# Attention scores of two heads side by side in 64-row halves, in six steps a group, with the value products in one piece

## What is computed

```python
# first layer, L0_attn and L0_ffn
xn = _layernorm(x, axis=-1)
qkv = jnp.einsum('btd,ed->bte', xn, w_qkv)          # 16 heads of 16 channels
scores = jnp.einsum('bqhd,bkhd->bhqk', q, k) * SCALE
scores = scores + causal_bias                       # -10000 above the diagonal
attn = jax.nn.softmax(scores, axis=-1)
out = jnp.einsum('bhqk,bkhd->bqhd', attn, v)
s = jnp.einsum('btd,ed->bte', out.reshape(b, t, D_OUT), w_out)
g = _silu(FFN(xn))                                  # gate, up, down with int weights
x = x + s * g
# second layer: a long convolution (by transforms) and a mixture of 20 experts with the best 2 of each token
```

## Time and profile before

| | us |
|---|---|
| median of 3 runs | 1039.91 (1037.98 to 1041.28) |
| the profiled execution | 1047.65, its span 1045.9 |
| PE busy | 954.6 (91%) |
| weight loads | 720.9 (69%) |
| DVE busy | 685.5 (66%) |
| ACT busy | 467.8 (45%) |
| POOL busy | 327.5 (31%) |
| mean granted clock of PE, as a share of full speed | 0.955 |

### The profile page before, as it was taken

How to read it: one execution, slowest core, us unless ns; L and a number is a source line. 1 busy time by engine, 2 the same in 40 slices (tenths; PEclk the granted TensorE clock), 3 DMA queues, 4 the chain that set the end, 5 groups by cost and what they waited for, 6 DMA issues and landing times.

```text
span 1045.9 us, 18938 instructions
## 1 busy us (share of the span) xinstructions
PE 954.6 (91%) x5844; PEld 720.9 (69%) x5844; DVE 685.5 (66%) x1451; ACT 467.8 (45%) x871; POOL 327.5 (31%) x605
## 2 busy tenths in 40 slices
PE   8789999999999999999999999775889995999996
PEld 6666865866776775775776766464657783888885
DVE  6474676667577577577577466444566334899998
ACT  4346456446455555545546545442222332444442
POOL 5223224513612613613614522513000044322220
PEclk9899999979999999999999997986999996999999
DMA  7955856335535534644544620456876652443431
GB/s 268 117 152 88 184 139 88 110 131 79 113 141 83 122 141 71 124 151 63 102 161 63 134 82 2 142 157 197 250 235 209 193 181 67 125 156 123 132 106 44
DMA packets 88187, 136.70 MB, mean 131 GB/s; under 512 B 9987, under 2 KB 63939, under 8 KB 86084
## 3 DMA queue, kind: packets, MB, share of 16 engines
q1 hardware_dynamic: 69636, 100.75, 40.0%
q0 software_dynamic: 6144, 16.79, 5.3%
q10 hardware_dynamic: 12352, 18.48, 5.1%
HBM read 79.36 MB, written 55.57 MB: 129 GB/s over the span
## 4 chain that ended last, share of the span: by engine, by line
PE 32%; issue 31%; POOL 13%; DVE 11%; SPq 4%; ACT 2%; DMA 2%; another core or an unknown queue 1%; POOLq 0%; DVEq 0%; ACTq 0%
POOL PT L1850 6%; PE PS L2032 5%; PE PS L1053 3%; PE PS L373 3%; PE PS L1067 3%; PE PS L1025 3%; POOL slots_in L664 3%; PE PS L317 3%; DVE tmp L481 3%; POOL h L1833 3%; PE PS L828 3%; SPq L1968 2%; PE PS L340 2%; POOL idle_p L1844 2%; SPq L1972 1%
## 5 line engine op out<-in xcount | busy, mean ns | idle before, releaser
L1562 DVE TENSOR_REDUCE Mneg<-PS 128x2 f32<-128x1024 f32 (+2 forms) x192 | 195.0, 1043 | 70.3 <-PE PS L1029 69.3
L1316 ACT ACTIVATE PT<-PS 128x512 f32<-128x512 f32 (+1 forms) x384 | 172.7, 530 | 122.8 <-PE PS L1053 120.8
L1025 PE MATMUL PS<-ks,qs 96*128 96x256 f32 (+3 forms) x512 | 122.0, 348 | 3.1 <-issue 2.1
L1053 PE MATMUL PS<-qs,ks 96*128 96x512 f32 (+3 forms) x512 | 122.2, 358 | 2.6 <-ACT PT L1316 1.5
L1844 POOL TENSOR_TENSOR idle_p<-neghalf 128x1 f32<-128x1 f32 x128 | 25.2, 196 | 307.7 <-ACT PT L1316 307.7
L1053 PEld LDWEIGHTS PS<-qs,ks 96*128 96x128 f32 x512 | 89.1, 195 | 37.5 <-ACT PT L1316 18.4
L828 PE MATMUL PS<-xnT,Wgu 128*128 128x512 f32 x384 | 103.3, 410 | 8.5 <-DVE h L1505 8.4
L2032 PE MATMUL PS<-Wes,xbT 128*128 x336 | 98.6, 405 | 3.4 <-issue 2.5
L1850 POOL TENSOR_SCALAR_AFFINE_SELECT PT<-PT 128x256 f32<-128x256 f32 x256 | 98.9, 410 | 0.0
L1067 PE MATMUL PS<-PT,V 128*32 128x512 f32 (+3 forms) x1024 | 88.0, 451 | 5.9 <-POOL PT L1850 4.9
L828 PEld LDWEIGHTS PS<-xnT,Wgu 128*128 128x128 f32 x384 | 69.9, 191 | 31.4 <-DVE h L1505 11.8
(11 more groups left out here) (239 smaller groups left out, 1604.3 us busy)
## 6 DMA issues: line engine op xcount, KB each, us to landing
qs<-qk_parts SPq DMA_DIRECT2D x96, 128.0 KB
ks<-qk_parts SPq DMA_DIRECT2D x96, 128.0 KB
slots_out<-yb ACTq DMA_DIRECT2D x28, 384.0 KB, 3.3
xb<-slots_in SPq DMA_DIRECT2D x83, 128.0 KB, 2.8
qk_parts<-qhl SPq DMA_DIRECT2D x16, 512.0 KB, 2.7
qk_parts<-khl SPq DMA_DIRECT2D x16, 512.0 KB, 3.1
xn2T_parts<-xn2T SPq DMA_DIRECT2D x8, 1024.0 KB, 4.9
xT<-xn2T_parts ACTq DMA_DIRECT2D x7, 1024.0 KB
```

The costliest lines, as they stand in the source:

```text
L1025: pe.matmul(out, qs[:, hd, P * qt:P * qt + P], ks[:, hd, 0:keys], start=n % a_bank == 0, stop=False, skip_group_check=True)
L1053: last = pe.matmul(PS[:, 4 + n, col:col + T - P * kt], ks[:, hd, P * kt:P * kt + P], qs[:, hd, P * kt:T], start=True, stop=True)
L1316: act.activation(PT[:, g % 2, j, 512 * n:512 * n + width], PS[:, 4 + n, 0:width], ACT.Exp, scale=SCALE).then_inc(S["exped"], 1)
L1562: dve.tensor_reduce(out=Mneg[:, 0, qt, heads[0]:heads[-1] + 1], in_=all_of, op=ALU.max, axis=AX.X, negate=True).then_inc(S["maxed"], 1)
```

## The change

It does five things.

1. `qs` and `ks` hold two heads, one above the other: head pair (0, 2) and (1, 3) of a group, the first in rows 0 to 49, the second in rows 64 to 113. KS is 50: the maxima stand right behind the 48 rows of parts. Every product of one head is issued beside that of the other (e = 0, 1), into another bank; both read 50 rows of their own half of the array.
2. The masks are added in halves too: the identity and the mask exist a second time with their halves exchanged (`halves_in`, four DMAs at the start that unit 0 of batch 0 waits for), and each bank gets two products over 64 rows.
3. The transposed scores of a group are six windows instead of four heads: window w writes one piece (512, 384+128 or 256 columns) of both heads of a pair, into two of three banks in rotation. A window waits until the exponentials before the preceding piece are done. ACT and POOL follow the new order.
4. The values of a group are one piece, after unit 5 and ahead of `maxima_as_rows`. Windows 4 and 5 of a group stand in the next step, after its units 0 and 1. The gate products of the next batch stand after the steps, between the windows of group 3.
5. DMAs are split in two, one for each half: `rows_of_maxima` issues two, `stack` fourteen (two of zeros, twelve of 64 KB). The clearing of `qs` by DVE and ACT at the start goes.

The diff, cut to what the text speaks of:

```diff
-KS = 96
+HALF_ROWS = 64
+PARTS = 48
+KS = 50
@@
-        qs = keep("qs", [KS, NH, T], F32R)
-        ks = keep("ks", [KS, NH, T], F32R)
+        qs = keep("qs", [P, NH // 2, T], F32R)
+        ks = keep("ks", [P, NH // 2, T], F32R)
@@ units: query tile, head pairs, keys
-        UNITS = ((3, (0, 1), 512), (3, (2, 3), 512), (2, (0, 1), 384), (2, (2, 3), 384),
-                 (1, (0, 1, 2, 3), 256), (0, (0, 1, 2, 3), 128))
+        UNITS = ((3, (0,), 512), (3, (1,), 512), (2, (0,), 384), (2, (1,), 384), (1, (0, 1), 256), (0, (0, 1), 128))
@@ SP, stack
                 for n, (dst, parts) in enumerate(((qs, Q_PARTS), (ks, K_PARTS))):
                     for blk, part in enumerate(parts):
-                        sp.dma_start(
-                            f(dst[HD * blk:HD * blk + HD, GH * g:GH * g + GH, :]),
...
+                        for e in range(2):
+                            row, src = HALF_ROWS * e + HD * blk, 64 * (g % 2) + 32 * e
+                            sp.dma_start(
+                                f(dst[row:row + HD, 2 * g:2 * g + 2, :]),
...
@@ SP, rows_of_maxima
-                sp.dma_start(f(qs[M0:M0 + 2, GH * g:GH * g + GH, :]), mrow[:, :]).then_inc(S["m_in"], 16)
+                for e in range(2):
+                    row = HALF_ROWS * e + PARTS
+                    sp.dma_start(f(qs[row:row + 2, 2 * g:2 * g + 2, :]), mrow[GH * NT * e:GH * NT * e + GH * NT, :]
+                                 ).then_inc(S["m_in"], 16)
@@ SP, after the four stacks of batch 0
+            for tile in (ident16, mask16):
+                for e in range(2):
+                    sp.dma_start(tile[HALF_ROWS * e:HALF_ROWS * e + HALF_ROWS, 1, :],
+                                 tile[HALF_ROWS * (1 - e):HALF_ROWS * (1 - e) + HALF_ROWS, 0, :]).then_inc(halves_in, 16)
@@ PE, unit
-                for n, (j, out) in enumerate(zip(heads, places)):
-                    hd = GH * g + j
-                    pe.matmul(out, qs[:, hd, P * qt:P * qt + P], ks[:, hd, 0:keys], start=n % a_bank == 0,
-                              stop=False, skip_group_check=True)
+                for x, pair in zip(pairs, places):
+                    for e, out in enumerate(pair):
+                        pe.matmul(out, qs[rows_of(e), 2 * g + x, P * qt:P * qt + P], ks[rows_of(e), 2 * g + x, 0:keys],
+                                  start=x == pairs[0], stop=False, skip_group_check=True)
@@ PE, transposed scores
-            def transposed_scores(b, g, j):
+            def transposed_scores(b, g, w):
+                x, n = w // 3, w % 3
+                c = piece_of(g, w, 0)          # 12 * g + 2 * w
...
+                else:
+                    pe.wait_ge(S["exped"], 48 * b + c - 1)
+                if w == 0:
+                    pe.wait_ge(S["m_in"], 32 * (NG * b + g + 1))
+                for kt, col in PIECES[n]:
+                    for e in range(2):
+                        last = pe.matmul(PS[:, 4 + (c + e) % 3, col:col + T - P * kt],
+                                         ks[rows_of(e), 2 * g + x, P * kt:P * kt + P],
+                                         qs[rows_of(e), 2 * g + x, P * kt:T], start=True, stop=True)
@@ PE, attention
+                for g in range(1, NG):
+                    for u in range(NU):
+                        unit(b, g, u)
+                        if u >= LATE:                                   # LATE = 2
+                            transposed_scores(b, g - 1, u - LATE)
+                        elif g > 1:
+                            transposed_scores(b, g - 2, WINDOWS - LATE + u)
+                        if g == 1 and u == 1 and not first:
+                            route_logits(b - 1)
+                    if g > 1:
+                        values(b, g - 2, range(NT))
+                    maxima_as_rows(b, g)
+                for w in range(WINDOWS - LATE, WINDOWS):
+                    transposed_scores(b, NG - 2, w)
+                if not last:
+                    gate_up(b + 1, (0,), (0,))
...
+                transposed_scores(b, NG - 1, 0)
...
+                values(b, NG - 2, range(NT))
...
+                values(b, NG - 1, range(NT))
```

More of the change, by code:

```diff
@@ L1410, in attention_scalar @@
             split_qk(0)
+            act.wait_ge(ident_in, 16)
+            act.activation(ident16[:, 0, :], ident[:, :], ACT.Copy).then_inc(id16, 1)
             for i in range(EARLY):
@@ L1556, in maxima @@
                 slot = slot_of(g, u)
-                qt, heads, keys = UNITS[u]
+                qt, pairs, keys = UNITS[u]
                 dve.wait_ge(S["unit"], NU * (NG * b + g) + u + 1)
```

227 lines of the change are left out of this document (105 added, 122 removed).

## The result

| | before | after |
|---|---|---|
| median | 1040.6 us (1037.98 to 1052.73, 4 runs) | 1089.41 us (1082.47 to 1094.98, 4 runs) |
| ratio after / before, 95% interval | | 1.0452 [1.0411, 1.0494] |
| the profiled execution, its span | 1047.65, 1045.9 | 1082.47, 1080.7 |
| mean granted clock of PE | 0.955 | 0.898 |

A forecast was written before the change was run, and what follows sets the result against it. PE, busy for 91% of the span, was taken to bound the kernel. 1047.65 + 16 (eight batches) + 7 (start) = 1071 us for the profiled execution, so 1063 for the median; 8-in-10 range 1025 to 1082.

The forecast's parts named there:

- +2.0 a batch, +16 for eight: Sum over a batch's steps and tail, 46.6 against 44.7 us, with group 0's units 0 to +0.4; +16 for eight batches.
- a rival of 0.07: Rival: PE's waits of 0.5 to 1.2 us a step bring a slow-clock spell each batch: +20 to 40, about 1095; chance 0.07.
- (a): In a step, the second maxima DMA takes 2.4 us, landing 3.1 us after the copy; window 0 waits until 3.15.
- about even: Rival: waits as in (a), but halved transfers land in 1.8 us, tail 0.5 shorter: +0.2 a batch, 1049 us; chance 0.14.
- (b): Windows 0 to 3 of a step wait for exponentials, 1.15, 1.2 and 0.9 us; window 3 through 6.8 us after the copy.
- (c): Values of a group in one piece in a step: 2.34 us, ending 9.15 us after the copy.
- (d): Turning the maxima to the end of the copy, at a step's end: 0.79 us, making the step 9.9 us.
- (e): The tail, from the last copy to the start of `heads_as_rows`: 17.4 us against 13.9, +3.5.
- faster: Rival: PE's savings count in the steps, -4.3 us a batch, -34, and with the start 1013 us; chance 0.19.
- The start: Unit 0 of batch 0 waits for the halves' four DMAs behind 56 others, 5.7 us late; +5 to +9, taken +7.

The follow-up runs named there:

- e19: Kernel after with 64-row pairs, the halves' DMAs early, four products ahead of group 1's turning, unit 2's scores three times in steps 2 and 3: 1047.71 us, 1.0002.
- e11: Kernel before with score and transposed score products over 128 rows in place of 96: 1039.23 us, 0.9966.
- e4: Kernel after with the four DMAs of the halves issued right behind the stack of group 0, not of group 3: 1081.16 us, 1.0315.
- e7: Kernel before with half of its score products and masks left out, so the layer is not computed: 1028.73 us, 0.9842.
- e8: Kernel before with score and transposed score products over 66 of the 96 rows: 1084.02 us, 1.0291.
- e6: Kernel after with each pair of score products of groups 1 to 3 given twice, the first overwritten: 1096.36 us, 1.0464.
- e9: Kernel after with the halves' four DMAs behind group 0's stack and score pairs of groups 1 to 3 given twice: 1087.3 us, 1.0408.
- e14: Kernel after with score pairs over 64 rows and each mask in one product over 128 rows, without halves and their four DMAs: 1085.38 us, 1.0418.
- e16: Kernel after with each mask in one product over 128 rows, no halves or their four DMAs, pairs over 50 rows: 1114.92 us, 1.0617.
- e10: Kernel after with each product of a score pair over 64 rows in place of 50, the added rows zeros on the query side: 1063.44 us, 1.0195.
- e1_fill_both: Kernel after with eight products ahead of group 1's turning and three, two and three ahead of tail waits, batches 0 to 6: 1080.1 us, 1.0385.

## Why the prediction was wrong, step by step

The direction was right and the size was not: 49 us where 23 were forecast, above the range (1082). The step that failed is the sum's "+2.0 a batch, +16 for eight", which stood on waits alone at full clock: the clock in the batches was put at nothing and left to a rival of 0.07. Measured, the waits cost about nothing and the clock 32 us in seven batches of the profiled execution.

- **(a) the DMAs.** Two, one behind the other, and window 0 waiting for the second: right. It came at T+2.69, not T+3.15: window 0 goes on about 2.0 us after the second's issue starts (421.72 + 0.66 for the first, window 0 at 424.38), where 2.4 was taken from the earlier trace rows. The Trainium skill, DMA: Bandwidth & Descriptors (Latency and other measured facts), has about 2.0; the trace agrees with it here. The rival "about even" had assumed 1.8, which was nearer than 2.4.
- **(b) the windows.** From window 0 to the end of window 3's own part it is 3.66 us (424.38 to 428.04) against 3.65 forecast: right as a sum, with one wait fewer.
- **(c), (d).** Values 2.17 us (2.34 forecast), turning to copy 0.79: right. With the shorter DMA, steps 1 to 3 are 9.02, 9.30 and 9.30 us at full clock (e19), where 9.4, 9.9 and 9.9 were forecast.
- **(e) the tail.** In batch 3 it ran at full clock from 348.20 to 365.30 us, 17.1 against 17.4: right.

```profile
365.30 1.96 PE L1155 MATMUL PS<-ident,OT 128*128 128x128 f32 x16 [0.54 <-ACT OT L1358]
```

- Taken together a batch at full clock costs 79.92 and 79.90 against 79.77 and 80.41 in e11, so between +0.15 and -0.5, not +2.0. The rival "even" had this right with its +0.2, though its own terms (0.6 less in each of three steps, 0.5 less in the tail) give -0.3 and 1045, not 1049. The rival "faster" had it wrong: PE's lost work did not shorten the batch.
- **The start** cost 6.05 us where 7 were taken: right in mechanism and size. Unit 0 waited for the four DMAs behind the 56, as forecast, and came 3.6 us late (53.25 against 49.69) where 5.7 were forecast; the other 2.5 came between unit 0 and the copy, with the clock at a half from 52.1 to 58.9 us, for which the forecast had 1 to 2 us. What e4 adds is that the doubled stacks cost nothing by themselves: with the four DMAs ahead of three of the four stacks, unit 0 starts before its old time.
- **The clock.** The seven periods took 591.2 us; at 79.90 each they would take 559.3. So 32 us in seven batches went to it, about all of the loss but the start in this execution; the three longer ones have a lower clock still. The rival named the place (a spell in each batch) and the price (20 to 40) well, and got 0.07 because "waits of this size stand in step 1 already, mostly without a fall". That argument looked for the cause in waits alone. The runs show two things that the change takes from PE besides: products (e7, half of them over the same 96 rows: low clock before 660 us from 37 to 116 us) and rows (e8). Over 96 rows the kernel before had spells in two of its eight batches (the earlier trace rows shows one), over 128 in none, over 66 in all, each in one profiled execution; no row of the trace of before showed the part of the rows, since all of its score products have the same 96. The Trainium skill, TensorE: Matmul & The Clock Gate (Part 1), has the gate follow how busy PE has been; here PE was busy for 16.98 of 17.20 us ahead of a fall in e8 and for the whole of the step after it, so that is not the whole of it.

Shown by experiment: products over 64 rows for 50 bring 1.0452 to 1.0195, the early DMAs that to 1.011, products ahead of PE's waits that to 1.0002. The products ahead of the turning run over 128 rows, so they shorten a wait and add rows and work at once; these runs don't say which of the three counts. Not settled: by what rule rows, products and waits together set the clock. Halved products over 96 rows changed much (e7) and doubled ones over 50 rows nothing (e6, e9), and whole masks brought more spells against theory R (e14, e16). The values in one piece and the DMAs in two were not tried by themselves.

## What to carry to other kernels

When PE's clock is part of the time, count what a change takes off the array as well as what it takes off PE's list, and give a fall of the clock a real price in the sum: a product over fewer rows costs the same time and can cost the clock. Rows of zeros took no more time in a product here and won 26 us (e10); try them before filling waits. And place DMAs that the first unit needs by when it needs them, not behind bulk transfers in the same queue.

## What the runs showed of the hardware

- Score products over 66, 96 and 128 rows in the same program: mean granted clock 0.89, 0.98 and 1.00 from 60 to 660 us in the profiled executions (1096.64, 1047.65 and 1036.09 us), 1.0291 [1.0231, 1.0351], 1 and 0.9966 [0.9929, 1.0003] in time, at the same time for a product (0.71 us for the two from 441.12 on, as in the earlier trace rows). 66 against 96 rows is clear of noise, 128 against 96 is not.
- Half of the products over the same 96 rows (e7): low clock before 660 us 116 us in place of 37.
- Between pairs over 64 rows, masks as products over all 128 rows cost 0.1 us more on either side than masks as pairs (0.64 against 0.44 us from scores to window).
- Two DMAs of 8 KB: both issued in 1.31 us; PE, which waited for both, went on about 2.0 us after the second's issue began.
- Eight products of 384 columns over 128 rows at the end of step 1, with more in the tail (e1_fill_both), took the spells out of step 2 in batches 1 to 3 and brought some into step 1 in batches 1, 2, 3 and 6.
